# A routed block cut in halves, and three shared chunks held back

## The reference

```python
x = x + 0.5 * ffn0(layernorm(x))   # 8 experts, top 2, width 176, and a shared expert of 352
x = x + mix(layernorm(x))          # time mixing and channel mixing
x = x + 0.5 * ffn0(layernorm(x))   # the second feed-forward, same weights
x = x + 0.5 * ffn1(layernorm(x))   # 32 experts, top 6, width 96, shared 192
x = x + linear_attention(layernorm(x))
x = x + 0.5 * ffn1(layernorm(x))
```

## Time and profile before

| what | us |
|---|---|
| median of 3 runs | 1507.77 |
| lowest, highest | 1500.41, 1521.2 |
| the profiled execution | 1497.55 |
| its span, first to last instruction | 1495.7 |
| busy PE, DVE, ACT, POOL | 1178.6, 743.8, 536.0, 596.8 |
| chain that ended last: PE, DVE, issue, unknown | 48%, 18%, 13%, 10% |

### The profile page before, as it was taken

The page is one execution under the profiler, slowest core; times in us unless marked ns, Lnnn a source line. Parts: engine busy times, 40 slices in busy tenths (PEclk is TensorE's granted clock), DMA queues, the critical chain, the costliest instruction groups (busy, mean ns, idle before and its releaser), DMA issues.

```text
span 1495.7 us, 20198 instructions
## 1 busy us (share of the span) xinstructions
PE 1178.6 (79%) x6031; PEld 960.0 (64%) x6031; DVE 743.8 (50%) x2333; ACT 536.0 (36%) x1012; POOL 596.8 (40%) x579
## 2 busy tenths in 40 slices
PE   4799988979989898854768998897755436988884
PEld 4677755666778676633557987875434225978784
DVE  5553465564546536413445555678644214633443
ACT  2323344554533234321413433442303115644442
POOL 3661352211124213674550155662453730045554
PEclk9789999998989999865868999898875667998897
DMA  9523439400002573331426687760121212676676
GB/s 331 211 72 107 143 96 308 141 1 0 1 29 107 206 260 119 117 114 64 173 76 216 195 241 237 219 191 4 60 79 41 105 53 63 198 208 205 204 223 191
DMA packets 125302, 209.81 MB, mean 140 GB/s; under 512 B 15296, under 2 KB 104768, under 8 KB 123328
## 3 DMA queue, kind: packets, MB, share of 16 engines
q1 hardware_dynamic: 100624, 141.38, 28.7%
q0 software_dynamic: 24576, 67.14, 14.4%
HBM read 129.29 MB, written 101.19 MB: 154 GB/s over the span
## 4 chain that ended last, share of the span: by engine, by line
PE 48%; DVE 18%; issue 13%; another core or an unknown queue 10%; ACT 6%; POOL 3%; DMA 1%; SPq 0%; DVEq 0%; POOLq 0%; ACTq 0%
PE ps L910 15%; PE ps L932 6%; PE ps L877 5%; PE ps L817 4%; PE ps L829 4%; PE ps L889 3%; PE ps L1093 2%; PE ps L1100 2%; ACT xnt L1360 1%; PE ps L927 1%; PE ps L1244 1%; DVE HL L2047 1%; POOL xd L638 1%; PE ps L925 1%
## 5 line engine op out<-in xcount | busy, mean ns | idle before, releaser
L653 POOL DMA_INDIRECT G<-yd,slot_of x256 | 253.1, 989 | 424.6 <-issue 189.3
L638 POOL DMA_INDIRECT xd<-xnt,slot_of x256 | 251.4, 982 | 224.4 <-DVE slot_of L1986 136.9
L910 PE MATMUL ps<-WE,xT 128*128 x1016 | 200.7, 343 | 5.6 <-issue 3.9
L2102 DVE TENSOR_TENSOR hid<-hid,ps 128x192 f32<-128x192 f32 (+2 forms) x168 | 65.4, 389 | 247.9 <-ACT hid L1551 198.1
L910 PEld LDWEIGHTS ps<-WE,xT 128*128 128x128 f32 x1016 | 174.0, 202 | 9.9 <-issue 9.7
L1522 ACT ACTIVATE xT<-ps 128x512 f32<-128x512 f32 (+1 forms) x168 | 99.2, 590 | 156.9 <-PE ps L877 121.6
L877 PE MATMUL ps<-ident,xd_in 128*128 128x128 f32 x664 | 108.2, 287 | 44.2 <-ACT xT L1522 24.0
L2081 DVE SCALAR_TENSOR_TENSOR XT<-G,wt,XT 128x256 f32<-128x256 f32 x256 | 123.8, 494 | 27.5 <-DMA G<-yd,slot_of 17.0
L1551 ACT ACTIVATE hid<-ps 128x192 f32<-128x192 f32 (+2 forms) x168 | 60.4, 359 | 192.1 <-PE ps L910 139.9
L877 PEld LDWEIGHTS ps<-ident,xd_in 128*128 128x128 f32 x664 | 84.5, 148 | 60.6 <-issue 37.0
L1379 ACT ACTIVATE S<-ps 128x512 f32<-128x512 f32 (+1 forms) x72 | 42.6, 592 | 179.1 <-PE ps L817 140.1
(11 more groups left out here) (245 smaller groups left out, 2173.6 us busy)
## 6 DMA issues: line engine op xcount, KB each, us to landing
xd_in<-xd SPq DMA_DIRECT2D x164, 256.0 KB
yd<-yo SPq DMA_DIRECT2D x164, 256.0 KB
WE<-w SPq DMA_DIRECT2D x8, 1280.0 KB
W0E<-w0e SPq DMA_DIRECT2D x1, 4864.0 KB
xd<-xnt,slot_of POOLq DMA_INDIRECT x256
G<-yd,slot_of POOLq DMA_INDIRECT x256
W0E<-w0e SPq DMA_DIRECT2D x1, 3040.0 KB
XT<-x_in SPq DMA_DIRECT2D x4, 512.0 KB, 6.1
```

The lines of the kernel that those rows point to most:

```text
L638: nc.gpsimd.indirect_dma_start(xd[f // 2][:, :], bass.IndirectOffsetOnAxis(ap=slot_of[:, t, k:k + 1], axis=0), xnt[:, t, :], None).then_in ...
L653: nc.gpsimd.indirect_dma_start(G[:, n % G_RING, :], None, yd[f // 2][0:min(ly.early[t][k] * 2, ly.TILES) * P, :], bass.IndirectOffsetOnAxi ...
L910: last = mm(dst, xT[:, q % 2, a, k, :], flat[:, bass.ds(expert[2 * q + a] + k * 2 * ly.H, 2 * ly.H)], start=(k == 0), stop=(k == KD - 1))
L2102: tt(hid[:, q % 2, 0:m, 0:ly.H], hid[:, q % 2, 0:m, 0:ly.H], src, ALU.mult).then_inc(TL.hid, 1)
```

## The change

It has two parts, and a rearrangement that they need.

The routing of f = 2 goes by units in place of blocks: `UNITS[2]` has five of them, tiles 0 and 1, tiles 2 and 3, and then blocks 1, 2 and 3. Unit 0 is routed at pairs 8 to 11 of the tile run (statistics, rows, turn with logits and choice, ranks and slots), unit 1 at pairs 10 to 13 and unit 2 at pairs 14 to 17. The routing functions `rank`, `score`, `chosen`, `slots`, the statistics and the rows take a unit of two or four tiles.

`HELD = 2`: for f = 1 block 2's three shared chunks leave the drain and join block 3's in `prepare2`, which thus begins with six held chunks. They are of kind "d0" there, with their own buffers. The routing of block 2 of f = 2 (unit 3) follows them. The tile run gathers all blocks (it stopped after three) and no longer waits for a block's shared sum when that block is a held one; the statistics of blocks 2 and 3 wait for those sums instead.

POOL's list gets another order, and weight group 7 is loaded with groups 0, 1 and 6 behind the held chunks, no longer within the tile run.

```diff
+HELD = 2
+UNITS = [[(NT * b, NT) for b in range(NB)] for _ in range(4)]
+UNITS[2][0:1] = [(0, NT // 2), (NT // 2, NT // 2)]
+ROUTED = [sum(len(u) for u in UNITS[:f]) for f in range(4)]
...
-    for b, banks in enumerate(((2, 2, 2), (2, 6, 2), (6, 2, 6), (2, 6, 2))):
-        add(("s", 1, b), "s0" if b < LATE else "d0", 1, b, SH0, banks)
+    for b, banks in enumerate(((2, 2, 2), (2, 6, 2), (2, 6, 2), (6, 2, 6))):
+        add(("s", 1, b), "s0" if b < HELD else "d0", 1, b, SH0, banks)
...
-DRAIN = [ch for b in range(LATE) for ch in RUN["s", 1, b][0]]
+DRAIN = [ch for b in range(HELD) for ch in RUN["s", 1, b][0]]
...
-                if 4 <= i < 9:
-                    expert_weights((2, 3, 4, 5, 7)[i - 4])
+                if 4 <= i < 8:
+                    expert_weights((2, 3, 4, 5)[i - 4])
...
-            for g in (0, 1, 6):
+            for g in (0, 1, 6, 7):
                 expert_weights(g)
...
-            for t in range(4):
-                gather(1, t)
-            inverse(F_NORM[2], 0)
-            for t in range(4, 8):
-                gather(1, t)
+            gather(1, 0)
+            gather(1, 1)
+            inverse_unit(2, 0)
+            gather(1, 2)
+            gather(1, 3)
+            inverse_unit(2, 1)
+            for t in range(4, 7):
+                gather(1, t)
             scatter_tile(2, 0)
-            inverse(F_NORM[2], 1)
+            gather(1, 7)
+            scatter_tile(2, 1)
             gather(1, 8)
+            inverse_unit(2, 2)
+            scatter_tile(2, 2)
             gather(1, 9)
-            scatter_tile(2, 1)
             gather(1, 10)
+            scatter_tile(2, 3)
             gather(1, 11)
-            scatter_tile(2, 2)
             gather(1, 12)
-            scatter_tile(2, 3)
             scatter_tile(2, 4)
...
             def route_ahead(i):
-                if i in (12, 16):
-                    route_turn(i // 4 - 3)
+                if i in (10, 12, 16):
+                    route_turn((10, 12, 16).index(i))
...
-                held = RUN["s", 1, LATE][0]
+                held = RUN["s", 1, 2][0] + RUN["s", 1, 3][0]
                 pe.wait_ge(TL.hid, PAIR0[2])
                 pe.wait_ge(TL.hT, PAIR0[2])
                 gate_up(held[0], taken_over(held[0]))
                 pe.wait_ge(TL.y, PAIR0[2])
-                route_turn(2)
-                gate_up(held[1], taken_over(held[1]))
-                route_logits(2)
-                down(held[0])
-                gate_up(held[2], taken_over(held[2]))
-                down(held[1])
-                route_rank(2)
-                down(held[2])
+                for k in range(1, 6):
+                    gate_up(held[k], taken_over(held[k]))
+                    down(held[k - 1])
+                route_turn(3)
+                down(held[5])
+                route_logits(3)
+                route_rank(3)
                 chunk(0)
                 chunk(1)
...
-                    if (f, t // NT) != (0, LATE):
+                    if f >= 2 or t // NT < (LATE, HELD)[f]:
                         dve.wait_ge(CK.sum, GROUP["s", f, t // NT] + 1)
...
-                held = RUN["s", 1, LATE][0]
-                offsets(F_NORM[2], 2, True)
-                prod(held[0])
-                low_hidden(held[0])
-                prod(held[1])
-                chosen(2, 2)
-                low_hidden(held[1])
-                prod(held[2])
-                low_hidden(held[2])
-                route_slots(2)
+                held = RUN["s", 1, 2][0] + RUN["s", 1, 3][0]
+                for k in range(4):
+                    prod(held[k])
+                    low_hidden(held[k])
                 finish(held[2])
+                dve.wait_ge(CK.sum, GROUP["s", 1, 2] + 1)
+                route_stats(3)
+                route_scaled(3, True)
+                for k in (4, 5):
+                    prod(held[k])
+                    low_hidden(held[k])
+                finish(held[5])
+                chosen(2, 3)
                 gathered_all(1, first)
-                route_stats(3)
+                route_slots(3)
+                dve.wait_ge(CK.sum, GROUP["s", 1, 3] + 1)
+                route_stats(4)
                 route_low(0)
                 route_low(1)
                 chunk(0)
```

More of the change, by code:

```diff
@@ L1017, in first_prepare, with route_turn @@
                     down(ch)
[L1019 to L1023, removed]
-                turn(F_NORM[2], b, xnt, route_banks(b)[0])
-            def route_logits(b):
-                pe.wait_ge(F_NORM[2].hi, b + 1)
+            def route_turn(u):
+                t0, n = UNITS[2][u]
+                if u:
+                    pe.wait_ge(RT.score, ROUTED[2] + u)
+                if t0 >= 2 * NT:
+                    pe.wait_ge(RT.slots, ROUTED[2] + u)
+                pe.wait_ge(F_NORM[2].rows, t0 + n)
+                bank = route_banks(t0 // NT)[0]
+                for k in range(KD):
+                    for a in range(n):
+                        last = nc.tensor.transpose(ps[:, bank + k, a * P:(a + 1) * P], xnt[:, t0 + a, k * P:(k + 1) * P], ident[:, :])
+                last.then_inc(F_NORM[2].turned, 1)
@@ L1028, in route_logits @@
+            def route_logits(u):
+                t0, n = UNITS[2][u]
+                pe.wait_ge(F_NORM[2].hi, u + 1)
                 E = LY[1].E
-                for a in range(NT):
+                for a in range(n):
+                    at = (t0 + a) % NT * P
                     for k in range(KD):
-                        last = mm(ps[:, route_banks(b)[0], a * E:(a + 1) * E], X2[b][:, k, a * P:(a + 1) * P], graw[1][:, k, :], start=(k == 0), stop=(k == KD - 1))
+                        last = mm(ps[:, route_banks(t0 // NT)[0], a * E:(a + 1) * E], X2[t0 // NT][:, k, at:at + P], graw[1][:, k, :],
+                                  start=(k == 0), stop=(k == KD - 1))
@@ L1275, in next_rank @@
                 if b:
-                    pe.wait_ge(RT.slots, NB * 3 + b)
+                    pe.wait_ge(RT.slots, ROUTED[3] + b)
                 rank(3, b, A_BANK)
@@ L1837, in moments, with moments_of @@
             def moments(b, src):
-                for a in range(NT):
+                moments_of(NT * b, NT, src)
+            def moments_of(t0, n, src):
+                for a in range(n):
                     last = nc.vector.bn_stats(st6[:, a, :], src[:, a, :])
@@ L1841, in moments @@
                 st.sync()
-                for a in range(NT):
-                    last = nc.vector.bn_aggr(mv[:, b * NT + a, :], st6[:, a, :])
+                for a in range(n):
+                    last = nc.vector.bn_aggr(mv[:, t0 + a, :], st6[:, a, :])
                 st.do(last)
@@ L1889, in zed, with chosen @@
                 tt(sc[:, tiles_of(b), 0:E], logit, smax[:, :].unsqueeze(2).broadcast_to([P, NT, E]), ALU.subtract).then_inc(RT.zed, 1)
-            def chosen(f, b):
+            def chosen(f, u):
                 ly = LAYER[f]
                 E, K, W8 = ly.E, ly.K, ly.E + 8
-                t0 = b * NT
-                dve.wait_ge(RT.score, NB * f + b + 1)
+                (t0, n), tiles = UNITS[f][u], unit_tiles(f, u)
+                dve.wait_ge(RT.score, ROUTED[f] + u + 1)
                 nc.vector.memset(idle[:, 0:1], 0.0)
-                for a in range(NT):
+                for a in range(n):
                     last = nc.vector.max(t8[:, a, :], sc[:, t0 + a, 0:W8])
```

280 lines of the change are left out of this document (154 added, 126 removed).

## The result

The changed kernel took 1529.41 us (median of 18 runs, 1517.81 to 1538.54), the kernel before 1515.06 us on the same chip (1495.24 to 1529.89): a ratio of 1.0141, interval 1.0115 to 1.0167. The ratio leaves out runs in a slower state (over 1.5% above the fastest of the same kernel: seven of the 18 before, none after), so it is larger than that of the two medians, 14.4 us or 1.0%. By the ratio the change costs 1.4%, some 21 us. The forecast was +6.5 us; the rival "the chunks crawl" had +22 us.

What follows compares the result with a forecast made beforehand. It took PE (48% of the chain) and results arriving late in POOL's unpaused bursts as the bound. Block 2's slots at 715 us put block 3's at 762.8 against 756.30: +6.5 us on 1507.77, 1514 us; range 1495 to 1528 us.

Steps and rivals of the forecast that it cites:

- the chunks crawl: Rival: the whole held run stays in a POOL burst, three more chunks cost 11.6 us each; +22 us, 1530 us, chance 0.16.
- The front: Start of the second tile run: no wait for block 2's shared chunks; 3 us gained, between 0 and 6.1 us.
- POOL's wait for block 2's slots: Sign in POOL's timeline of the third feed-forward: this wait grows from 17.32 us to about 30 us.
- the price of the held chunks: Before block 2's slots: three added chunks at 5 us each, 15 us; slots at about 715 us instead of 706.16.
- the end of the second burst: POOL's unpaused stretch from gather 11, at 635 us, through 34 operations ends at 684 us instead of 688.84 us.
- my first burst: POOL's unpaused stretch in the tile run: 597 to 628 us instead of to 620.44, delaying block 1's score by 7.6 us.
- 13 us for two halves: Tile run: routing block 0 in two halves costs 13 us against 9.6 us whole, so 3.5 us lost.
- a score that starts inside a burst: Sign against the forecast: a block's score starting during POOL's unpaused work; block 1's score was expected near 628 us.
- Block 3's stretch: From block 2's slots at 715 us: 24 scatters to 747 us, score 1.3 us later, block 3's slots at 762.8 us.
- The bursts stop hurting: Rival: store waits between scatters let held chunks run freely, 7 us each; -12 us, 1496 us, chance 0.22.
- it does not do what it says: Rival: POOL's first scatters start no sooner or its 17.32 us wait absorbs all shifts; within 3 us of 1508, chance 0.12.
- The rule on the clock gate: Held chunks: PE's throttled state is the default, so added chunks would cost some 8 us each, 9 us more in sum.

Runs made afterwards that it cites:

- four readings of the kernel before: The kernel before and three later kernels identical to it up to the fourth feed-forward; block 2's slots at 197.5 to 200.6 us from the mark.
- e1: The kernel after with block 0 routed whole again and POOL's list as before, keeping six held chunks; ratio to the kernel before 1.012.
- e3: The kernel after with POOL waiting for the last held gate and up before scattering tiles 5 to 7; ratio to the kernel before 1.0039.
- e12: The kernel before, four scatters in flight, with six already met waits behind every scatter's wait; ratio to the kernel before 1.0101.

## Why the prediction was wrong

**Right.** The front: 3 us gained, measured 3.0. POOL's wait for block 2's slots, "about 30 us": 33.49. The first slots at about 582 us: the slots' first half was there at 583.28 us. 24 scatters in 31 to 32 us: 30.0 + 1. The direction was right too. The first scatter, also forecast for 582 us, came only at 589.62 us, behind gather 6.

**The step that failed: the price of the held chunks.** The forecast priced three added chunks at 15 us, by the rows behind a burst, let one more fit inside the burst, and took off 5 us because the burst would end sooner: block 2's slots at 715 us, 8.8 us later. Against the mark they came 18.9 us later, and 15.8 to 18.9 us later than in the four readings of the kernel before. The chunks alone (e1) make 215.4 - 197.5 = 17.9 us of that. In e1 the burst ends at 689.05 - 511.63 = 177.4 us from its mark, close to the forecast's 175.8, and the slots are late all the same. So the earlier end of the burst was no gain to be taken off, and the crawl inside the burst was the row to price by. With POOL silent beside the chunks (e3) the slots come at 196.3 us.

**Behind it, a wait put at nothing: the end of the second burst.** I shortened the burst by 5 us (684 against 688.84). Against the mark it ended 7.6 us later than forecast, and 2.7 us later than before, where the four readings of the kernel before lie between 180.6 and 186.8 us. The forecast had 24 operations "without a wait" from the second scatter tile to gather 11. But the inverse of block 1 stands among them, and it waited 7.50 us for DVE's statistics. From gather 11 on the forecast was close: 695.45 - 645.28 = 50.2 us against 49. The wait comes from my first burst. I had it run from 597 to 628 us and hit block 1's score. It started at 589.62 us, ran to 610 us, and hit the pairs. PE's matmuls behind pair 14's gate and up waited 11.30 us, and DVE's work on the hidden rows, ahead of those statistics, 15.12 us:

```profile
613.26 0.52 DVE L2157 TENSOR_TENSOR hid<-hid,ps 128x352 f32<-128x352 f32 x1 [15.12 <-ACT hid L1591]
```

Pair 15 thus starts 9.4 us late against the mark (614.71 - 512.09 = 102.6 against 601.41 - 508.20 = 93.2). Until there the halves cost nothing: from pair 10 to pair 14 are 593.29 - 568.46 = 24.8 us, against 592.04 - 567.01 = 25.0 us before. So the term "13 us for two halves" was too high, and the price of a burst in the tile run stood at the wrong place. Block 1's score starts at 631.66 us, in the middle of POOL's unbroken work from 617.51 to 639.20 us. The forecast had named just this, a score that starts inside a burst, as a sign of being wrong: that a score arrives when the burst is over doesn't always hold. The first held chunk came 2.2 us late, where I had 8.1, but as said above this mark is not steady enough to build on.

**Block 3's stretch.** I let it stay as it was and even shorten by 2.3 us (762.8 - 715 = 47.8 us against 50.1). It took 53.2 us, though its burst was 3.4 us shorter than before. The silu of the third of the eight shared chunks of f = 2 now waited in it (11.39 us, up to 763.09 us), so that the score came 8.3 us behind the burst's end at 759.88 us instead of 1.3.

**The sum along POOL's list.** The burst's end is 7.6 us off, the way from there to block 2's slots 2.5 us (33.5 against 31), block 3's stretch 5.4 us: 15.5 us, which with the forecast's 6.5 gives the 22 of the profiles. That 31 us came so close is partly luck: with the same six chunks it is 38.4 us in e1, whose burst ends 6 us sooner while its slots come only 1 us sooner. The first two parts can't be taken one by one.

**The rival "the chunks crawl"** was the right one. It gave +22 us by another count (35 less 5 less one chunk; with its own 11.6 us for that chunk it would be 18) and from the point where the burst reaches 695 us. The burst ended at 695.45 us, but this was not what decided, as e1 shows. As I read the timelines, a burst lets through three or four of these chunks, however many stand in it (three in e1). Before, block 2's rows, turn and logits used the rest of that time; with six chunks they come after it, behind the chunks that are left. My chance of 0.16 was too low: I had the row that shows two gate and ups taking 35 us, and priced the new chunks by the rows after the burst all the same. "The bursts stop hurting" and "it does not do what it says" fell.

Two readings of the forecast were off as well. Block 2's slots add up to 706.2 - 4.8 + 15 = 716.3 us and not 715. And the list of POOL's waits leaves out one inside the burst of 627 to 689 us, before gather 15 (POOL's timeline before):

```profile
663.64 0.94 POOL L653 DMA_INDIRECT G<-yd,slot_of  x1 [3.15 <-DMA yd<-yo]
```

POOL stands still from 660.49 us. DVE's drain that had waited 11.40 us starts at 661.23 us, in that very pause. So the trace of before already had a late result that came not with the burst's end but in a short pause of POOL.

The rule on the clock gate (the Trainium skill, TensorE: Matmul & The Clock Gate, Part 1: the clock gate) would have made the sum 9 us higher, 15.5 us in all, nearer to the truth. But the way was another one: the granted clock in the second burst was 0.74, not 0.61 as in the earlier trace rows, and the first three gate and ups in it ran in 2.9 us each. The time went by between them. Only the fifth, right behind the burst, took 5.76 us. The windows view of the kernel after, columns as in the earlier trace rows:

```profile
639.00:695.45 56.45, 35.98 (x142) 26.36 (x142) 17.39 (x50) 9.25 (x16) 34.25 (x35) 0.74 0.30 100
695.45:728.90 33.45, 19.17 (x94) 15.49 (x94) 19.37 (x77) 13.95 (x19) 0.00 (x0) 0.70 0.36 142
```

**Open.** Why PE's hand-offs are late while POOL issues indirect transfers without ever waiting. Transfers that load instructions are no candidate that the trace supports: in the 35 us in which DVE waits in the kernel before, 1185 to 1220 us, the view of the DMA queues has this one queue alone, and its engines are three quarters idle.

```profile
## 3 DMA queue, kind: packets, MB, share of 16 engines
q0 software_dynamic: 1161, 3.15, 25.2%
```

Whether PE itself works on unseen, or stands, is not settled either: between its single steps no other engine's record names a cause. Nor is it settled why two in flight cures so much in the fourth and nothing in the third, where gathers stand between the scatters and were not capped; capping these wasn't tried. And e3 moves scatters and leaves gathers, so it shows what the scatters do beside the chunks, not which part of a scatter does it: POOL's issue, the transfer or its landing.

## What to carry to other kernels

Before moving work from a quiet stretch into one where another queue is busy, price it by the worst row of that stretch, not by the nearest quiet one, and ask how many such pieces the stretch lets through at all. Lay the busy times of the engines side by side and look at long waits that nobody explains: if they all end when one engine pauses, that engine is the thing to change first. Here one number, the scatters in flight, was worth 3.6%, where the reordering cost 1.4%.

## What the runs showed of the hardware

- While POOL issues indirect scatters 1.27 us apart without a wait on a landing, results of PE reach DVE and ACT late. In the last burst of the kernel before, DVE stands idle for 32.95 us (32.95 us after, 32.96 us with three in flight) and starts 30 us behind PE's recorded end (1188.54 and 1218.49 us), 4.1 us behind the last scatter. ACT and DVE hand over to each other within 0.8 us in such stretches.
- In such a stretch PE also starts matmuls one by one, 0.70 us or a multiple of it apart.
- A late result can come in a short pause of POOL: in the one of 3.15 us in the kernel before (661.23 us), and at its first falter in e12 (1211.85 us). They don't always wait for the end (block 1's score after, 631.66 us).
- A small slowing of POOL helps a little: in the last burst 1.266 us apart costs a wait of 33 us, 1.329 us apart breaks it up (0.9945). Two in flight at 1.392 us gives 0.9816, not by pace alone. Six waits that are met already leave most scatters of the last burst at 1.26 to 1.27 us.
- One scatter at a time costs 2.67 us each, 1.70 us of it waiting for the landing. ACT then has one unexplained wait above 2.5 us in the profile between 490 and 820 us (6.81 us), and DVE none.
